# Cross attention of a perceiver block: text probabilities and weighted sums carried in the same turn and the same return transfer as the image probabilities, queries made per batch

## The chip, the cores and the metric

One Trainium2 chip, one of its cores. The metric is the device time of the whole program in microseconds (us); the kernel before has a median of 2453.11 us over 3 runs (2441.91 to 2453.33). The program computes a whole two-layer block; the change touches one stage of it, `cross_attention`, the image and text cross attention of the second layer.

## The reference, cut to what matters

```python
# x: 16 batches x 64 tokens x 256; context: 16 x 1601 x 256, the first 77 rows are text
def _attend(q, k, v):
    sim = jnp.einsum('bihd,bjhd->bhij', q, k) * SCALE        # 16 heads of 64, SCALE = 1/8
    attn = jax.nn.softmax(sim, axis=-1)
    out = jnp.einsum('bhij,bjhd->bihd', attn, v)
    return out.reshape(B, N, H * D)
q = (x @ Wq).reshape(B, N, HEADS, DIM_HEAD)
out = _attend(q, ctx_txt @ Wk, ctx_txt @ Wv)                  # 77 text keys
out = out + _attend(q, ctx_img @ Wk_ip, ctx_img @ Wv_ip)      # 1524 image keys
return out @ Wo + bo
```

Two softmaxes over two sets of keys, each normalised by itself, are added, and the sum goes through one output projection. All is fp32.

## The kernel before

The 1024 tokens are 8 tiles of 128, a tile is 2 batches of 64, and 16 heads are 8 pairs. The loop runs over 128 steps g; a step is one batch and one pair of heads (128 rows: 2 heads x 64 tokens), 16 steps to a tile. The image keys and values are never made: the query is taken through the key weights (`key_side`, result `a_hi` + `a_lo`), multiplied with the raw context (`ct`, split in two parts that one pass can hold exactly), and the probabilities are multiplied with the raw context rows (`cn`), after which the 256-wide sums go through the value weights (`value_side`).

Each engine has its own program, in order, and they meet in semaphores. In step g:

- PE (TensorE) computes the text scores and the image scores of g (L2237, L2248 to L2250: 18 matmuls of 508 columns), turns the normalised text probabilities of g-1 (`turn_text`, L2257) and the sums of g-3 (`turn_sums`, L2279), makes the key side of g+1 (L2228), then the sums of g-2 (L2271: 12 blocks, each three matmuls of 256 columns: `pt_hi` with both parts of `cn`, `pt_lo` with the first), and the value side of g-3 (L2293, L2295). The scores of g+1 wait until ScalarE has read the scores of g (`exp_done`).
- DVE (VectorE) takes the maxima (L2449, L2450), makes `a_lo` (L2437), turns the 128x1536 probabilities within 32x32 blocks in four instructions (L2466), normalises the text (L2470), splits the moved probabilities (`pt_lo`, L2478) and keeps the sums (L2482).
- ACT (ScalarE) computes the exponentials (L2402, L2405), copies `pt_hi` from `prob_moved` (L2414), and keeps what PE leaves in three PSUM banks that go round (`t_ps`).
- POOL (GpSimd) splits the context of the next batch as it is loaded.
- SP issues the transfers. A block turned within 32x32 is not yet turned as a whole; the rest of the turn is a trip through memory. Four stores (L2147) go out, one after each of the four DVE instructions, each from all 128 partitions in runs of 1536 bytes; then four returns (L2152), each into 32 partitions, again in runs of 1536 bytes. The landing place `prob_moved` has two buffers, so the returns of g wait for the splits of g-2. After them SP issues one load of context and, in some steps, weights and text keys and values.

Every 16 steps comes a boundary: the queries of the next tile (L2218: 16 fp32 products with 128 columns, 32 matmul records) are made between score steps, and key side and scores wait for them. Two steps later the finished tile goes through the output projection (`project`, L2307). `wq` and `wo` share one place in SBUF (`w_shared`) and are loaded in turn.

Of the kernel before, what the change touches and what calls it, by code (L numbers as in the profile page):

```python
# [22 lines left out]
P = 128  # L23
D = 256
# [2010 lines left out]
def cross_attention(nc, k, src, first):  # L2035
# [8 lines left out]
    RUN = IB * QR  # L2044
    with ExitStack() as ctx:
# [19 lines left out]
        prob = sb("prob1", [P, TXT + IB * P])  # L2065
        blocks = sb("prob_blocks", [P, Q, IB, QR])
# [3 lines left out]
        pt_txt = [sb(f"pt_txt{s}", [P, P]) for s in range(3)]  # L2070
        pairs = sb("pairs1", [P, 10, 2])
        top, bias, total, inv = ([pairs[:, at + s] for s in range(n)] for at, n in ((0, 2), (2, 2), (4, 3), (7, 3)))
        o = sb("o1", [P, D])
        ot = sb("ot1", [P, C, P])
# [5 lines left out]
        k_in, v_in, v_used = sem("k_txt_in"), [sem(f"v_txt_in{b}") for b in range(2)], sem("v_txt_used")  # L2080
# [4 lines left out]
        turned, moved_in, split_done = sem("prob_turned"), [sem(f"prob_moved_in{s}") for s in range(2)], sem("prob_split")  # L2085
        t_done = [sem(f"t1_done{j}") for j in range(RING)]
        t_kept = [sem(f"t1_kept{j}") for j in range(RING)]
        a_hi_kept, pt_hi_kept, txt_normed = sem("a_hi_kept"), sem("pt_hi_kept"), sem("txt_normed")
        summed, half_summed, inv_done, sums_kept = sem("summed1"), sem("half_summed1"), sem("inv1_done"), sem("sums1_kept")
        q_zeroed, pad_zeroed = sem("q_zeroed"), sem("prob_pad_zeroed")  # L2090
        stored = [sem(f"prob_stored{m}") for m in range(Q)]
# [7 lines left out]
        def boundary(g):  # L2099

            return g % STEPS == STEPS - 1 and g < N - 1

        def projects(g):

            return g // STEPS - 1 if g % STEPS == 2 and g >= STEPS else None
# [5 lines left out]
        def _(sp):  # L2111
# [29 lines left out]
            for g in range(N):  # L2141
# [12 lines left out]
                if g // PAIRS1 + 1 < NB:  # L2154
                    load(g // PAIRS1 + 1, g % PAIRS1)
                if n == 0 and i:
                    sp.wait_ge(scored, g)
                    load_keys(i, 1)
                    sp.wait_ge(queried, i + 1)
                    sp.dma_start(wo, src["wo1"]).then_inc(wo_in, 16)  # L2160
                if n == 4 and i:
                    sp.wait_ge(v_used, 2 * i)
                    load_values(i, 1)
                if n == 5 and 1 <= i < NT - 1:
                    sp.wait_ge(projected, i)
                    sp.dma_start(wq, src["wq1"]).then_inc(wq_in, 16)
                if n == 12 and i < NT - 1:
                    sp.wait_ge(scored, i * STEPS + 12)
                    load_keys(i + 1, 0)
                if n == 13 and i < NT - 1:  # L2170
                    sp.wait_ge(v_used, 2 * i + 1)
                    load_values(i + 1, 0)

        @block.gpsimd
        def _(pool):
# [14 lines left out]
            nc.gpsimd.memset(prob[:, TXT + IMG:], 0.0).then_inc(pad_zeroed, 1)  # L2190
# [8 lines left out]
        def _(pe):  # L2199
# [11 lines left out]
            def queries(t):  # L2211

                for side in range(2):
                    bank = use()
                    for j in range(4):
                        p = 4 * side + j
                        for c in range(C):
                            last = nc.tensor.matmul(t_ps[bank][:, j * P:(j + 1) * P], wq[:, c, p * P:(p + 1) * P],  # L2218
                                                    k.h_t[:, c, t * P:(t + 1) * P], start=c == 0, stop=c == C - 1)
                    last.then_inc(t_done[bank], 1)  # L2220
                return ring.place(2), ring.place(1)
# [31 lines left out]
            def turn_text(g):  # L2253

                bank = use()
                pe.wait_ge(txt_normed, g + 1)
                nc.tensor.transpose(t_ps[bank][0:TXT, 0:P], prob[:, 0:TXT], k.ident).then_inc(t_done[bank], 1)  # L2257

            def sums(g):
# [15 lines left out]
            def turn_sums(g):  # L2275
                bank = use()
                pe.wait_ge(sums_kept, g + 1)
                for c in range(C):
                    last = nc.tensor.transpose(t_ps[bank][:, c * P:(c + 1) * P], o[:, c * P:(c + 1) * P], k.ident)  # L2279
                last.then_inc(t_done[bank], 1)  # L2280
                return ring.place(1)

            def value_side(g):
# [3 lines left out]
                if p == 0:  # L2287
                    pe.wait_ge(v_in[b], 16 * i + 16)
                heads = [(t_ps[bank][r * S:(r + 1) * S, 0:S], slice((2 * p + r) * HD1, (2 * p + r + 1) * HD1),
                          slice(r * S, (r + 1) * S)) for r in range(2)]  # L2290
                for c in range(C):
                    for out, cols, rows in heads:
                        nc.tensor.matmul(out, wv[:, c, cols], ot[:, c, rows], start=c == 0, stop=False)  # L2293
                for out, cols, rows in heads:
                    last = nc.tensor.matmul(out, v_txt[0:TXT, b, cols], pt_txt[g % 3][0:TXT, rows],  # L2295
# [3 lines left out]
            def project(t):  # L2299
                kept(ring.place(1))  # L2300
                if t < NT - 1:
                    pe.wait_ge(wo_in, 16 * (t + 1))
# [9 lines left out]
            q_places = queries(0)  # L2312
            pe.wait_ge(wk_in, 16)
            for place in q_places:
                kept(place)
            a_place = key_side(0)
            for g in range(N + 3):
# [10 lines left out]
                if boundary(g):  # L2328
                    if g > STEPS:
                        pe.wait_ge(wq_in, 16 * (g // STEPS) + 16)  # L2330
                    q_places = queries(g // STEPS + 1)
                elif g < N - 1:
                    a_place = key_side(g + 1)
                if 2 <= g <= N + 1:
                    sums(g - 2)
                if boundary(g):
                    for place in q_places:
                        kept(place)
                    a_place = key_side(g + 1)
                if g >= 3:  # L2340
                    if g == 3:
                        pe.wait_ge(wv_in, 16)
                    kept(ot_place)
                    value_side(g - 3)
                if projects(g) is not None:
                    project(projects(g))
# [9 lines left out]

        def keep_queries(eng, copy, mine, ring):

            for side in range(2):
                bank, count = ring.next()  # L2360
                if side == mine:
                    eng.wait_ge(t_done[bank], count)
                    for r in range(2):
                        rows = slice(r * HD1, (r + 1) * HD1)
                        last = copy(q[rows, 4 * side:4 * side + 4, :, r, :],
                                    t_ps[bank][rows, :].rearrange("p (j b n) -> p j b n", j=4, b=2))
                    last.then_inc(t_kept[bank], 1)
# [9 lines left out]
        def _(act):  # L2377
# [9 lines left out]

            act.wait_ge(q_zeroed, 1)
            keep_queries(act, copy, 0, ring)
            keep_a(0)  # L2390
            for g in range(N + 3):
                if 1 <= g <= N:
                    keep(act, copy, ring, pt_txt[(g - 1) % 3][0:TXT, :], TXT, P)
                if g >= 3:
                    keep(act, copy, ring, flat(ot), P, D)
                if not boundary(g) and g < N - 1:
                    keep_a(g + 1)
                if g < N:
                    act.wait_ge(bias_done, g + 1)
                    if g:  # L2400
                        act.wait_ge(turned, Q * g)
                    nc.scalar.activation(prob[:, TXT:M].rearrange("p (j m) -> p j m", j=SB), s_ps[:, 1:4, 0:SBLK],  # L2402
# [625 lines left out]
```

## Time and profile before

| | |
|---|---|
| median of 3 runs | 2453.11 us (2441.91 to 2453.33) |
| profiled execution | 2435.73 us, of it the span 2433.6 us |
| first to last score step in the span | 624.1 to 2000.7 us |
| PE busy over the span | 2160.2 us (89%) |
| DVE, ACT, POOL busy | 65%, 38%, 36% |
| DMA engines, mean share | 48.1% for the queue that SP issues on |

PE's records overlap, so what a piece of its work takes is read from the start of one record to the start of the next. The cross attention takes 1.4 ms of the 2.4 ms. Outside it nothing is changed.

### The profile page before, as it was taken

How to read it: one execution, taken by the hardware profiler on the slowest of the kernel's cores; microseconds unless marked ns; L12 is line 12 of the kernel's file. 1: busy time of each engine (PE TensorE's matmuls, PEld its weight loads, DVE VectorE, ACT ScalarE, POOL GpSimd, SP SyncE). 2: the span in 40 equal slices, each digit the busy share in tenths (PEclk: the TensorE clock that was granted, in tenths of full speed). 3: DMA queues.
4: the chain of work that ended last, by engine and by line, in shares of the span. 5: the costliest groups of instructions: out<-in, count | busy, mean ns of one | idle time of the engine just before them, and what ended most of it. 6: DMA issues, size and time to landing. Idle time of an engine off the chain costs nothing. (4 is left out here: it accounts for less than half of the span.)

```text
span 2433.6 us, 37422 instructions
## 1 busy us (share of the span) xinstructions
PE 2160.2 (89%) x13637; PEld 1726.1 (71%) x13637; DVE 1570.4 (65%) x2756; ACT 925.0 (38%) x1869; POOL 877.5 (36%) x535
## 2 busy tenths in 40 slices
PE   5878877796699999999999999999999997787897
PEld 3445545464598889888898998998998994334684
DVE  4179934333577677677677677777776763795554
ACT  1166611210244344344344444444443443452331
POOL 1066412431343333243343333343333300362455
PEclk8989977798899999999999999999999998798898
DMA  5800002511476677677676777776776656001364
GB/s 159 169 16 14 8 1 88 230 50 57 145 200 184 185 218 205 185 217 206 185 217 180 226 202 208 198 207 199 202 211 186 194 156 248 4 0 44 98 148 114
DMA packets 229957, 362.99 MB, mean 149 GB/s; under 512 B 41920, under 2 KB 197824, under 8 KB 225168
## 3 DMA queue, kind: packets, MB, share of 16 engines
q1 hardware_dynamic: 223008, 342.08, 48.1%
q0 software_dynamic: 6768, 18.49, 3.2%
q8 instruction: 115, 1.88, 0.3%
q14 instruction: 66, 0.54, 0.1%
HBM read 234.97 MB, written 125.50 MB: 148 GB/s over the span
## 5 line engine op out<-in xcount | busy, mean ns | idle before, releaser
L2271 PE MATMUL img_ps<-cn,pt_hi 128*128 128x256 f32 (+1 forms) x3072 | 569.7, 287 | 3.0 <-DVE pt_lo L2478 3.0
L2271 PEld LDWEIGHTS img_ps<-cn,pt_hi 128*128 128x128 f32 (+1 forms) x3072 | 477.3, 191 | 3.2 <-issue 3.2
L2271 PE MATMUL img_ps<-cn,pt_lo 128*128 128x256 f32 (+1 forms) x1536 | 435.9, 284 | 0.0
L2466 DVE STREAM_TRANSPOSE prob_blocks<-prob 128x384 f32<-128x384 f32 x512 | 250.6, 547 | 183.8 <-ACT prob L2402 175.9
L2248 PE MATMUL s_ps<-ct,a_hi 128*128 128x508 f32 x768 | 315.7, 411 | 0.0
L2249 PE MATMUL s_ps<-ct,a_hi 128*128 128x508 f32 x768 | 304.2, 396 | 0.0
L2250 PE MATMUL s_ps<-ct,a_lo 128*128 128x508 f32 x768 | 304.0, 396 | 0.0
L2001 POOL TENSOR_SCALAR ct<-staged 128x762 fp32r<-128x762 f32 x64 | 136.8, 2138 | 439.6 <-DMA staged<-in_ctx_t 312.5
L2271 PEld LDWEIGHTS img_ps<-cn,pt_lo 128*128 128x128 f32 (+1 forms) x1536 | 292.6, 190 | 0.0
L2478 DVE TENSOR_TENSOR pt_lo<-prob_moved,pt_hi 128x768 fp32r<-128x768 f32 x256 | 277.9, 1124 | 9.4 <-ACT pt_hi L2414 9.2
L2001 POOL TENSOR_SCALAR cn<-staged 128x768 fp32r<-128x768 f32 x64 | 137.4, 2147 | 376.5 <-DMA staged<-in_ctx_n 293.4
L2379 ACT ACTIVATE pt_txt<-t_ps 77x128 f32<-77x128 f32 x128 | 34.9, 273 | 577.0 <-PE t_ps L2257 577.0
L2402 ACT ACTIVATE prob<-s_ps,pairs 128x1524 f32<-128x1524 f32 x128 | 196.5, 1535 | 136.7 <-DVE pairs L2453 136.7
L2414 ACT ACTIVATE pt_hi<-prob_moved 128x768 fp32r<-128x768 f32 x256 | 214.7, 842 | 62.7 <-PE img_ps L2271 46.7
L2450 DVE TENSOR_REDUCE pairs<-s_ps 128x1 f32<-128x1524 f32 x128 | 222.0, 1735 | 0.0
L2250 PEld LDWEIGHTS s_ps<-ct,a_lo 128*128 128x128 f32 x768 | 146.5, 191 | 32.6
L2249 PEld LDWEIGHTS s_ps<-ct,a_hi 128*128 128x128 f32 x768 | 147.6, 192 | 27.3
L2248 PEld LDWEIGHTS s_ps<-ct,a_hi 128*128 128x128 f32 x768 | 147.3, 192 | 27.5
L1736 PE MATMUL up_ps_b<-up_all_m,xt_b 128*128 x436 | 152.4, 481 | 1.3 <-issue 0.5
L2449 DVE TENSOR_REDUCE pairs<-s_ps 128x1 f32<-128x77 f32 x128 | 30.4, 238 | 182.9 <-PE s_ps L2250 182.9
L2003 POOL TENSOR_TENSOR cn<-staged,cn 128x768 fp32r<-128x768 f32 x64 | 125.6, 1963 | 5.3
L1684 POOL DMA_INDIRECT rows_b<-rows_m,token_m x86 | 84.7, 984 | 113.4 <-POOLq L1467 64.1
(370 smaller groups left out, 3712.9 us busy)
## 6 DMA issues: line engine op xcount, KB each, us to landing
prob_rows<-prob_blocks SPq DMA_DIRECT2D x512, 192.0 KB, 2.1
prob_moved<-prob_rows SPq DMA_DIRECT2D x512, 192.0 KB, 3.6
staged<-in_ctx_n SPq DMA_DIRECT2D x64, 384.0 KB, 4.7
staged<-in_ctx_t SPq DMA_DIRECT2D x64, 381.0 KB, 4.7
up_all_m<-in_up SPq DMA_DIRECT2D x8, 2048.0 KB, 12.8
down_all_m<-in_down SPq DMA_DIRECT2D x8, 1024.0 KB, 23.4
sums_m<-y_b SPq DMA_DIRECT2D x63, 128.0 KB, 2.2
w_shared<-in_wq SPq DMA_DIRECT2D x7, 1024.0 KB, 7.3
```

What stands on the lines that cost most here:

```text
L1736: last = nc.tensor.matmul(up_ps[j % 2][:, own], xt[j % 2][:, c, :], m.up[:, bass.ds(expert, 1), c, own].rearrange("p a h -> p (a h)"), sta ...
L2001: nc.gpsimd.tensor_scalar(hi, piece, 1.0, None, ALU.mult).then_inc(first.hi_done, 1)
L2003: nc.gpsimd.tensor_tensor(lo, piece, hi.bitcast(F32), ALU.subtract).then_inc(done, 1)
L2248: nc.tensor.matmul(out, a_hi[:, c, :], ct[b][:, 0, c, cols], start=c == 0, stop=False)
L2249: nc.tensor.matmul(out, a_hi[:, c, :], ct[b][:, 1, c, cols], start=False, stop=False)
L2250: last = nc.tensor.matmul(out, a_lo[:, c, :], ct[b][:, 0, c, cols], start=False, stop=c == C - 1)
L2271: last = nc.tensor.matmul(img_ps[:, 0:D], left[0:n, j, :], rows[0:n, right, j, :], start=j == 0 and at == 0, stop=j == IB - 1 and at == 2)
L2402: nc.scalar.activation(prob[:, TXT:M].rearrange("p (j m) -> p j m", j=SB), s_ps[:, 1:4, 0:SBLK], ACT.Exp, bias=bias[g % 2][:, 1:2], scale= ...
L2414: nc.scalar.activation(in_quarters(pt_hi, h), by_block(moved[(g - 1) % 2], h), ACT.Copy).then_inc(pt_hi_kept, 1)
L2450: nc.vector.tensor_reduce(top[g % 2][:, 1:2], s_ps[:, 1:4, 0:SBLK], mybir.AxisListType.XY, ALU.max).then_inc(topped, 1)
L2466: nc.vector.transpose(blocks[:, m], source[:, m]).then_inc(turned, 1)
L2478: nc.vector.tensor_tensor(in_quarters(pt_lo, h), by_block(moved[(g - 1) % 2], h), in_quarters(pt_hi, h).bitcast(F32), ALU.subtract).then_i ...
```

## The change

What it does:

- `prob` has 15 blocks of 128 columns in place of the 77 text columns and 12 image blocks: 12 of image probabilities, one of text probabilities (77 of its 128 columns), two of the 256-wide sums. Text and sums in it are those of two steps earlier.
- One DVE instruction turns all 1920 columns. The four stores now take a quarter of the partitions each (32 partitions, four runs of 1920 bytes from each), all after that instruction. One return brings everything to 128 partitions, 7680 bytes to each. `prob_moved` has one buffer in place of two; the return of g waits for the splits of g-1 and the value side of g-4.
- PE's `turn_text` and `turn_sums` go, with ACT's copies of their results. The value side reads text and sums from `prob_moved`, a step later than before, and waits for the return of the step before its own. 
- The sums take two matmuls to a block in place of three: `pt_hi` with both parts of `cn` (512 columns), `pt_lo` with the first. ACT scales the second half (`o_part`) and DVE adds. ACT, not DVE, normalises the text.
- Queries are made per batch (64 columns, 16 products) at the end of steps 6 and 13 of a tile, and ACT keeps them. `wq` and `wo` are loaded in halves, in steps 4 and 5 and in 14 and 15.

```diff
-    RUN = IB * QR
+    TXT_AT, O_AT = IB, IB + 1
+    BUNDLE = IB + 1 + C
+    RUN = BUNDLE * QR
+    LAG = 3
...
-        block_rows = nc.dram_tensor("prob_rows", (2, Q, P, RUN), F32).ap()
-        moved = [sb(f"prob_moved{s}", [P, Q, IB, QR]) for s in range(2)]
+        block_rows = nc.dram_tensor("prob_rows", (2, Q, QR, Q, RUN), F32).ap()
+        moved = sb("prob_moved", [P, Q, BUNDLE, QR])
...
+        def queries_of(g):
+
+            i, _, _, n = parts(g)
+            return {6: 2 * i + 1, 13: 2 * i + 2 if i < NT - 1 else None}.get(n) if g < N else None
...
         # sync
                 if g >= 2:
-                    sp.wait_ge(moved_in[s], 16 * Q * (g // 2))
-                for m in range(Q):
-                    sp.wait_ge(turned, Q * g + m + 1)
-                    sp.dma_start(block_rows[s, m], blocks[:, m].rearrange("p j r -> p (j r)")).then_inc(stored[m], 16)
-                if g >= 2:
-                    sp.wait_ge(split_done, 2 * (g - 1))
-                for m in range(Q):
-                    sp.wait_ge(stored[m], 16 * (g + 1))
-                    sp.dma_start(moved[s][m * QR:(m + 1) * QR].rearrange("c a j r -> c a (j r)"),
-                                 block_rows[s, m].rearrange("(a c) f -> c a f", a=Q)).then_inc(moved_in[s], 16)
+                    sp.wait_ge(moved_in, 16 * (g - 1))
+                sp.wait_ge(turned, g + 1)
+                for a in range(Q):
+                    sp.dma_start(block_rows[s, :, :, a].rearrange("m c f -> c m f"),
+                                 blocks[a * QR:(a + 1) * QR].rearrange("c m j r -> c m (j r)")).then_inc(stored[a], 16)
+                if g:
+                    sp.wait_ge(split_done, 2 * min(g, N))
+                if g > LAG:
+                    sp.wait_ge(valued, g - LAG)
+                for a in range(Q):
+                    sp.wait_ge(stored[a], 16 * (g + 1))
+                sp.dma_start(moved[:].rearrange("p a j r -> p (a j r)"),
+                             block_rows[s].rearrange("m c a f -> (m c) (a f)")).then_inc(moved_in, 16)
...
         # tensor
-                        for at, (left, right) in enumerate(((pt_hi, 0), (pt_hi, 1), (pt_lo, 0))):
-                            last = nc.tensor.matmul(img_ps[:, 0:D], left[0:n, j, :], rows[0:n, right, j, :],
-                                                    start=j == 0 and at == 0, stop=j == IB - 1 and at == 2)
+                        nc.tensor.matmul(img_ps[:], pt_hi[0:n, j, :], rows[0:n, :, j, :], start=j == 0, stop=False)
+                        last = nc.tensor.matmul(img_ps[:, D:2 * D], pt_lo[0:n, j, :], rows[0:n, 0, j, :],
+                                                start=False, stop=j == IB - 1)
...
             def value_side(g):
+                pe.wait_ge(moved_in, 16 * (g + LAG + 1))
...
-            for g in range(N + 3):
+            for g in range(N + LAG + 2):
...
-                if 1 <= g <= N:
-                    turn_text(g - 1)
-                if g >= 3:
-                    ot_place = turn_sums(g - 3)
...
+                if LAG + 1 <= g <= N + LAG:
+                    value_side(g - LAG - 1)
+                    head_place = ring.place(1)
+                if queries_of(g) is not None:
+                    if g >= STEPS:
+                        pe.wait_ge(wq_in, 32 * (g // STEPS) + 16)
+                    q_place = queries(queries_of(g))
...
         # vector
-                    for m in range(Q):
-                        if g:
-                            dve.wait_ge(stored[m], 16 * g)
-                        nc.vector.transpose(blocks[:, m], source[:, m]).then_inc(turned, 1)
+                    if g:
+                        for a in range(Q):
+                            dve.wait_ge(stored[a], 16 * g)
+                    nc.vector.transpose(blocks[:], prob[:].rearrange("p (j m c) -> p m j c", j=BUNDLE, m=Q)).then_inc(turned, 1)
```

## Rows read from the trace of the kernel before

**Rows 1.** The page, part 1: busy time (share of span) xinstructions.

```profile
PE 2160.2 (89%) x13637; PEld 1726.1 (71%) x13637; DVE 1570.4 (65%) x2756; ACT 925.0 (38%) x1869; POOL 877.5 (36%) x535
```

**Rows 2.** Windows (A:B length, busy by engine, PEclk, DMA share, GB/s), steps.

```profile
660.00:2000.00 1340.00, 1318.02 (x9770) 1191.89 (x9770) 976.63 (x1647) 582.20 (x1258) 489.95 (x241) 0.99 0.69 199
```

**Rows 3.** Waits of 660 to 2010: who waited for whom, total us, times, longest.

```profile
PE s_ps L2237 <- issue: 11.8, 7, 1.9
DVE prob_blocks L2466 <- ACT prob L2402: 172.8, 125, 1.7
```

**Rows 4.** Timeline of PE, one step: start, us, what, count.

```profile
1199.71 0.45 PE L2237 MATMUL s_ps<-k_txt,q 128*128 128x77 f32 x2
1199.95 0.47 PE L2248 MATMUL s_ps<-ct,a_hi 128*128 128x508 f32 x1
...
1204.16 0.27 PE L2257 MATMUL t_ps<-small,prob 128*77 128x128 f32 x1
...
1204.49 0.61 PE L2228 MATMUL t_ps<-q,wk 128*128 128x128 f32 x4
1204.85 0.49 PE L2271 MATMUL img_ps<-cn,pt_hi 128*128 128x256 f32 x2
...
1209.33 0.45 PE L2293 MATMUL t_ps<-ot,wv 128*64 128x64 f32 x8
...
1209.83 0.45 PE L2237 MATMUL s_ps<-k_txt,q 128*128 128x77 f32 x2
```

**Rows 5.** Timeline of PE around a boundary and around a projection.

```profile
1136.04 0.45 PE L2237 MATMUL s_ps<-k_txt,q 128*128 128x77 f32 x2
1140.86 3.74 PE L2218 MATMUL t_ps<-h_t,w_shared 128*128 128x128 f32 x32
1152.19 0.68 PE L2237 MATMUL s_ps<-k_txt,q 128*128 128x77 f32 x2 [1.53 <-issue]
...
1186.00 3.84 PE L2307 MATMUL t_ps<-w_shared,head_out 128*128 128x128 f32 x32 [0.55 <-ACT head_out L2379]
```

**Rows 6.** Timeline of VectorE in the same step as rows 4.

```profile
1200.24 1.82 DVE L2478 TENSOR_TENSOR pt_lo<-prob_moved,pt_hi 128x768 fp32r<-128x768 f32 x2
1204.52 1.74 DVE L2450 TENSOR_REDUCE pairs<-s_ps 128x1 f32<-128x1524 f32 x1
1208.14 1.96 DVE L2466 STREAM_TRANSPOSE prob_blocks<-prob 128x384 f32<-128x384 f32 x4 [1.36 <-ACT prob L2402]
```

**Rows 7.** Timeline of SP in the same step: stores, then returns.

```profile
1208.80 1.81 SPq L2147 DMA_DIRECT2D prob_rows<-prob_blocks  x4
1210.73 1.84 SPq L2152 DMA_DIRECT2D prob_moved<-prob_rows  x4
```

**Rows 8.** Tile view, single issues: store at 1208.80, returns at 1210.73 and 1212.27.

```profile
DMA to landing us min/median/max: 1.9/1.9/1.9
...
DMA to landing us min/median/max: 3.3/3.3/3.3
...
DMA to landing us min/median/max: 4.4/4.4/4.4
```

**Rows 9.** Windows: stores alone; returns alone; a context load and a weight load.

```profile
1209.75:1211.75 2.00, 2.00 (x15) 1.66 (x12) 1.96 (x5) 0.65 (x2) 1.92 (x2) 1.00 1.03 368
...
1213.25:1215.25 2.00, 2.00 (x15) 1.75 (x14) 1.44 (x4) 0.60 (x2) 0.00 (x0) 1.00 0.90 199
...
1226.75:1228.00 1.25, 1.25 (x13) 1.25 (x12) 0.27 (x1) 1.25 (x1) 0.00 (x0) 1.00 0.97 397
```

**Rows 10.** DMA issues: tensors, count, KB each, median us from issue to landing.

```profile
staged<-in_ctx_n SPq DMA_DIRECT2D x64, 384.0 KB, 4.7
...
w_shared<-in_wq SPq DMA_DIRECT2D x7, 1024.0 KB, 7.3
...
x_sb<-in_x SPq DMA_DIRECT2D x1, 1024.0 KB, 5.9
...
wv<-in_wv SPq DMA_DIRECT2D x1, 1024.0 KB, 4.7
```

**Rows 11.** Score steps by line (first and last start), and the last projection.

```profile
L2237 PE MATMUL s_ps<-k_txt,q x256: 232/275/497, 624.1 to 2000.9; 128*128 128x77 f32 x128
...
2029.48 3.84 PE L2307 MATMUL t_ps<-w_shared,head_out 128*128 128x128 f32 x32 [0.32 <-ACT head_out L2379]
```

More of the change, by code:

```diff
@@ L2097, in parts @@
             return i, n // PAIRS1, n % PAIRS1, n
[L2099 to L2101 removed]
+        def queries_of(g):
+            i, _, _, n = parts(g)
+            return {6: 2 * i + 1, 13: 2 * i + 2 if i < NT - 1 else None}.get(n) if g < N else None
         def projects(g):
[L2105 removed]
+            return g // STEPS - 1 if g % STEPS == LAG + 1 and g >= STEPS else None
         def half(h):
@@ L2209, in kept, with queries @@
                 pe.wait_ge(t_kept[place[0]], place[1])
[L2211 to L2221, printed above, removed]
+            def queries(b):
+                bank = use()
+                for p in range(PAIRS1):
+                    for c in range(C):
+                        last = nc.tensor.matmul(t_ps[bank][:, p * S:(p + 1) * S], wq[:, c, p * P:(p + 1) * P],
+                                                k.h_t[:, c, b * S:(b + 1) * S], start=c == 0, stop=c == C - 1)
+                last.then_inc(t_done[bank], 1)
+                return ring.place(1)
             def key_side(g):
@@ L2311, in _ @@
             pe.wait_ge(wq_in, 16)
-            q_places = queries(0)
+            q_place = queries(0)
             pe.wait_ge(wk_in, 16)
-            for place in q_places:
-                kept(place)
+            kept(q_place)
             a_place = key_side(0)
-            for g in range(N + 3):
+            for g in range(N + LAG + 2):
                 if g < N:
@@ L2355, in flat @@
             return a[:].rearrange("p c n -> p (c n)")
[L2357 to L2367, printed above, removed]
         def by_block(tile, h):
@@ L2386, in keep_a, with keep_queries @@
                 nc.scalar.activation(flat(a_hi), t_ps[bank][:, 0:D], ACT.Copy).then_inc(a_hi_kept, 1)
+            def keep_queries(b):
+                bank, count = ring.next()
+                act.wait_ge(t_done[bank], count)
+                act.sem_inc(queried, 1)
+                for r in range(2):
+                    rows = slice(r * HD1, (r + 1) * HD1)
+                    last = copy(q[rows, :, b % 2, r, :], t_ps[bank][rows, :].rearrange("p (j n) -> p j n", j=PAIRS1))
+                last.then_inc(t_kept[bank], 1)
             act.wait_ge(q_zeroed, 1)
-            keep_queries(act, copy, 0, ring)
+            keep_queries(0)
             keep_a(0)
[L2391 to L2396, printed above, removed]
+            for g in range(N + LAG + 2):
+                if g < N - 1:
                     keep_a(g + 1)
+                if projects(g) is not None:
+                    ring.next()
+                    ring.next()
                 if g < N:
@@ L2440, in _ @@
             nc.vector.memset(q[:], 0.0).then_inc(q_zeroed, 1)
-            dve.wait_ge(q_zeroed, 1)
-            keep_queries(dve, copy, 1, ring)
-            dve.sem_inc(queried, 1)
+            ring.next()
             keep_a_lo(0)
             dve.wait_ge(pad_zeroed, 1)
-            for g in range(N + 3):
+            for g in range(N + LAG + 2):
                 if g < N:
@@ L2484, in _ @@
-                if boundary(g):
-                    keep_a_lo(g + 1)
-                if g >= 3:
-                    ring.next()
                 if projects(g) is not None:
-                    if g == STEPS + 2:
+                    if g == STEPS + LAG + 1:
                         dve.wait_ge(bo_added, 1)
@@ L2496, in _ @@
                     dve.sem_inc(projected, 1)
+                if 1 <= g <= N:
+                    for h in range(2):
+                        dve.wait_ge(pt_hi_kept, 2 * (g - 1) + h + 1)
+                        nc.vector.tensor_tensor(in_quarters(pt_lo, h), by_block(moved, h),
+                                                in_quarters(pt_hi, h).bitcast(F32), ALU.subtract).then_inc(split_done, 1)
+                if 2 <= g <= N + 1:
+                    dve.wait_ge(part_kept, g - 1)
+                    dve.wait_ge(turned, g + 1)
+                    nc.vector.scalar_tensor_tensor(out=prob[:, O_AT * P:], in0=img_ps[:, 0:D],
+                                                   scalar=inv[(g - 2) % 3][:, 1:2], in1=o_part[:], op0=ALU.mult,
+                                                   op1=ALU.add).then_inc(sums_kept, 1)
+                if LAG + 1 <= g <= N + LAG:
+                    ring.next()
+                if queries_of(g) is not None:
+                    ring.next()
 class ScanWeights:
```

158 lines of the change are left out of this document (65 added, 93 removed).

## The prediction

> **What bounds the kernel now.** I read the page's busy shares first, then the windows, then the waits, then one step in the timeline of each engine. PE is busy 89% of the span [rows 1], and between 660 and 2000 us 1318.02 of 1340 us, at 0.99 of its clock [rows 2]. What it waits for there is small: 11.8 us in 7 places [rows 3], the tile boundaries. So the score loop is bound by PE's own stream of matmuls. An ordinary step lasts 1209.83 - 1199.71 = 10.12 us [rows 4]. A boundary step lasts 1152.19 - 1136.04 = 16.15 [rows 5], 6.03 more: 3.7 for the queries, the rest waiting. A projection adds 3.84 and a wait of 0.55, less 0.1 of overlap: 4.3 [rows 5]. A tile of 16 steps is 16 x 10.12 + 6.03 + 4.3 = 172.3 us. The 127 steps from 624.1 to 2000.7 us [rows 11] are 7.9 tiles.
>
> VectorE has slack: it waits 172.8 us in 125 steps before it turns the probabilities [rows 3]. The transfers of a step are done long before anybody needs them: the stores go out at 1208.80, the returns at 1210.73 [rows 7], and the last, issued at 1212.27, lands 4.4 later [rows 8], at 1216.67; ScalarE first wants them in the next step, after its exponentials, near 1218.4. That slack is what the change spends.
>
> **What PE saves.** The turns of text and sums take 1204.49 - 1204.16 = 0.33 us [rows 4]; they go. The 36 matmuls of the sums take 1209.33 - 1204.85 = 4.48, 0.124 each. The 508-column matmuls come at (1204.16 - 1199.95)/18 = 0.234 [rows 4], so a block of 512 and 256 columns costs 0.236 + 0.124 = 0.360 in place of 0.373: 0.16 over 12 blocks. PE's own work per step becomes 10.12 - 0.33 - 0.16 = 9.63. The queries leave the boundary and its 2.3 us of waiting; their work stays. With 64 columns a record costs between half of today's 3.74/32 = 0.117 [rows 5] and all of it, if the weight load sets the pace: 1.9 to 3.7 us for each batch. I take 2.4, since a projection record with its whole 128 columns is no quicker than 0.12.
>
> **What joins the path.** The value side of step k-4 stands at the end of PE's step k, and now waits for the return of k-1. PE is in order, so the scores of k+1 stand behind it. Nobody waited there before. I follow one bundle from the start S of its score step:
> - DVE starts to turn at S + 1208.14 - 1199.71 = S + 8.43 [rows 4, 6]. That is unchanged.
> - The turn: 1920 columns for 1536. Four pieces take 1.96 [rows 6], so 1.25 x 1.96 = 2.45; by the reduction's rate (1524 columns in 1.74, rows 6) 2.19. I take 2.3. Before, the first store left after one quarter, at 1208.80; now all four leave after the whole, 0.12 behind it: S + 10.85.
> - The stores, W. A store of 192 KB from 128 partitions lands 1.9 after issue [rows 8]; the window of stores alone moves 368 GB/s [rows 9], so 0.53 of that is data and 1.37 is latency. Each new store has 240 KB (245,760 bytes), but leaves only 32 partitions. No row shows such a store. Its two neighbours: stores from 128 partitions (0.67 us each at 368 GB/s, W = 1.37 + 4 x 0.67 = 4.05), and today's returns, which touch 32 partitions of SBUF: 199 GB/s in a window of their own [rows 9], and by their landings (1216.67 - 1214.03)/3 = 0.88 us for 192 KB [rows 7, 8]. Scaled to 240 KB that is 1.10 to 1.24; with 1.17, W = 1.37 + 4.68 = 6.05. I take 6.05: the 32 partitions are what the new stores share with that row, and HBM as such isn't what slows those returns, since context and weights come in at 397 GB/s [rows 9].
> - The return, L: 960 KB to all partitions. The nearest loads of 1024 KB land after 4.7 to 7.3 us [rows 10], the 7.3 with others queued ahead. The queue is empty when this one is issued, because SP has waited for the stores: 4.5, range 4.0 to 5.9.
> - From landing to the next scores: 0.1 and the value side, 1209.83 - 1209.33 = 0.50 [rows 4]. With 0.1 for SP's wait: 0.7 in all.
>
> So the scores of step g+2 can't start before S + 10.85 + W + L + 0.7, and two steps last 11.55 + W + L. With 6.05 and 4.5 that is 22.1: T = 11.05 us a step, against 9.63 of PE work and 10.12 today. The gain on PE becomes a wait of 1.4 us in front of every value side.
>
> A rule of the Trainium skill speaks against these stores. The page "SBUF — State Buffer", section "Door 1: The DMA port swizzle", says that a transfer's bandwidth depends on how many of SBUF's 16 ports its partitions reach, that 32 neighbouring partitions reach 8, and gives 189 GB/s at 1 MiB for them. By its figure (an estimate from that page) a store would have 1.30 us of data, W would be 6.6 and T 11.3. The trace agrees for transfers into 32 partitions, with its 199 GB/s [rows 9]; no run here shows it for transfers out of them.
>
> **Per tile, the extras.** Queries come right behind the value side and so on the path of one of the two alternating chains, twice a tile: 2.4 in all. Those of step 6 also wait for the second half of `wq`, which SP issues in step 5 behind return and context load: about 2 on one chain, so 1.0. A projection of 3.84 eats the slack of 1.4 and costs 2.4 on one chain and 1.0 on the other: 1.7. The halves of `wq` and `wo` (1.4 us of data at 368 GB/s, four times) and text keys and values are queued behind a context load, and the next stores behind them, by about 1.0 and 0.6: half of the sum, 3.2. Together 8. A tile is 16 x 11.05 + 8 = 184.8, 12.5 more than 172.3; over 7.9 tiles +99 us.
>
> **The end.** From the last scores (2000.7, rows 11) to the last projection's end it is 33 us. Now four bundles must still go round: the first lands at 10.85 + 6.05 + 0.1 + 4.5 = 21.5, and each further one 8.45 later (turn and stores, because one `prob_blocks` holds the next turn until the stores have landed): 46.9, plus value side and projection 5: 52. That is +19.
>
> DVE loses the text scaling and gets 0.3 more of turn and a little more for the sums: nothing, since it waits anyway. ACT gets two small operations and loses two: nothing; but what it does after its wait for the return (splits, sums, values) comes 1.7 to 3 us after the landing, and the next sums are wanted 5.5 after it, so this stays hidden, with POOL's collisions too. The single buffer costs nothing by itself, since the splits are done about 3 us after a landing and the stores of the next bundle land 5.5 after it.
>
> **Sum.** The profiled execution has 2435.7 us (span 2433.6). 2435.7 + 99 + 19 = 2554. The median of the runs is 17 above that execution, the fastest run 6. I predict 2560.
>
> **Rivals.**
> - The stores run at the full rate: W = 4.05, L = 4.5, T = 10.05. A tile is 160.8 + 10 (less slack, so queries and projection show more) = 170.8; -1.5 x 7.9 = -12; the end +13. With L at 4.0 T is 9.8 and the whole -30. Time 2410 to 2455, say 2425. For it: no row shows a slow store. Against: the returns' 199 GB/s. From W + L = 8.7 (T = 10.12) down it decides. Chance 0.17.
> - The change does what its instruction counts say: PE stays the bound, T = 9.65, a tile 154.4 + 8.7 = 163, -9.2 x 7.9 = -73, the end +8: 2375. It needs W + L under 7.8, less than 4.05 + 4.0. Against it is the sum of its two fastest rows. Chance 0.07.
> - The added wait is larger than my sum: PE's pauses let the clock go down, or the loads of context (4.7 alone, rows 10) and weights meet the stores in each step and W + L reaches 12.5: T = 12, a tile 202, +235: 2690. Half of that, 2620, is nearer. For it: 7.3 where a load had company. Against: the clock stayed at 0.99 over boundaries with 2 us of waiting [rows 2, 5]. Chance 0.12.
> - The forecast: 0.64, by itself 2500 to 2600.
>
> About 0.5% (12 us) is what a measurement of this kernel tells from no change. Faster: 0.22 (second rival, most of the first); same: 0.05; slower: 0.73. The range is 2415 to 2630.
>
> **What would show it.** Right: PE waits about 1.4 us in nearly every step before L2293's successor, released by the DMA of `prob_moved`; steps near 11 us; in the stores' window about 210 GB/s with the last landing 6 us after the first issue; the return landing in 4.5; no wait at the boundary; PE's busy share down, not the number of GB/s. Wrong: stores of 240 KB that land 0.7 us apart, or a value side that never waits and steps of 9.7; or a PE that waits elsewhere, at the scores for the exponentials or at the sums for the splits, which would mean that ACT or DVE, behind the return, sets the step.

## The result, and the profile after

The changed kernel takes 2693.12 us (median of 4 runs, 2687.21 to 2701.5), the kernel before 2452.89 (4 runs). The ratio is 1.0994, 95% interval 1.0948 to 1.104: 9.9% slower. The forecast was 2560 us, 4.4% slower, with a range that ended at 2630. The sign, the wait that joins the path and the length of the round trip at the full clock came out as forecast; the size did not.

The waits of PE in the score loop. Each row: who waited for whom, total us, times, longest. It answers to [rows 3].

```profile
PE t_ps L2288 <- DMA prob_moved<-prob_rows: 154.0, 62, 5.0
PE t_ps L2226 <- DMA w_shared<-in_wq: 14.0, 7, 2.2
PE img_ps L2272 <- DVE prob L2471: 6.2, 4, 2.5
```

L2288 is the value side. Where PE waited 11.8 us before, at boundaries, it now waits 154 us for the return. Two steps of PE's timeline, against [rows 4]:

```profile
1215.34 0.45 PE L2288 MATMUL t_ps<-prob_moved,wv 128*64 128x64 f32 x8
...
1215.84 0.45 PE L2245 MATMUL s_ps<-k_txt,q 128*128 128x77 f32 x2
...
1227.80 0.45 PE L2288 MATMUL t_ps<-prob_moved,wv 128*64 128x64 f32 x8 [2.65 <-DMA prob_moved<-prob_rows]
...
1228.30 0.45 PE L2245 MATMUL s_ps<-k_txt,q 128*128 128x77 f32 x2
```

This step lasts 12.46 us in place of 10.12, and 2.65 of it is one pause ahead of the value side. VectorE's turn and SP's timeline in the same step, against [rows 6, 7]:

```profile
1214.55 2.18 DVE L2448 STREAM_TRANSPOSE prob_blocks<-prob 128x1920 f32<-128x1920 f32 x1 [1.36 <-ACT prob L2385]
```

```profile
1216.80 2.71 SPq L2150 DMA_DIRECT2D prob_rows<-prob_blocks  x4
1222.91 0.34 SPq L2158 DMA_DIRECT2D prob_moved<-prob_rows  x1
```

The turn takes 2.18 us. From the first store's issue to the return's, which waits for the last store, it is 6.11 us in this step; over the steps of the loop the median is 5.98, with the last store landing 5.90 after the first issue. The page's rows of the transfers (count, KB each, median us to landing):

```profile
prob_rows<-prob_blocks SPq DMA_DIRECT2D x524, 240.0 KB, 4.1
prob_moved<-prob_rows SPq DMA_DIRECT2D x131, 960.0 KB, 4.8
```

And the window of the loop (length, busy by engine, PEclk, DMA share, GB/s), against [rows 2]:

```profile
660.00:2220.00 1560.00, 1393.41 (x8121) 1178.34 (x8120) 908.27 (x1128) 590.48 (x1268) 514.87 (x240) 0.92 0.66 203
```

PEclk is the line that the forecast got wrong. 0.92 over 1560 us means, with two levels of 1.2 and 2.4 GHz, 0.08 x 1560 / 0.5 = 250 us at half clock, where the kernel before had some 27 by the same sum (0.01 x 1340 / 0.5), and 17 by the single stretches of its trace. It comes in two ways. In the ordinary steps the wait mostly falls into every second step only, and the scores of the step after it often start at half clock. The step that begins at 1239.82 has 1.72 us of waiting just ahead of it. PE, the clock over its first scores, and VectorE's turn:

```profile
1239.33 0.45 PE L2288 MATMUL t_ps<-prob_moved,wv 128*64 128x64 f32 x8 [1.72 <-DMA prob_moved<-prob_rows]
...
1239.82 0.45 PE L2245 MATMUL s_ps<-k_txt,q 128*128 128x77 f32 x2
```

```profile
1240.30:1243.60 3.30, 3.30 (x9) 2.57 (x9) 2.64 (x3) 1.21 (x4) 3.18 (x2) 0.50 0.94 275
```

```profile
1249.83 2.18 DVE L2448 STREAM_TRANSPOSE prob_blocks<-prob 128x1920 f32<-128x1920 f32 x1 [1.36 <-ACT prob L2385]
```

The turn starts 10.01 us after the scores, where it starts 8.42 after them in a step at the full clock (1214.55, with scores from 1206.13). The round trip starts later by that much, and PE itself does not wait in this step, because its slow scores have used up the time. Where it hurts most is step 6 of a tile, the one with queries and their weights just reloaded:

```profile
1297.54 0.45 PE L2245 MATMUL s_ps<-k_txt,q 128*128 128x77 f32 x2
...
1309.32 0.45 PE L2288 MATMUL t_ps<-prob_moved,wv 128*64 128x64 f32 x8 [2.46 <-DMA prob_moved<-prob_rows]
...
1311.92 7.09 PE L2226 MATMUL t_ps<-h_t,w_shared 128*128 128x64 f32 x32 [2.02 <-DMA w_shared<-in_wq]
1318.80 0.65 PE L2245 MATMUL s_ps<-k_txt,q 128*128 128x77 f32 x2
```

```profile
1311.90:1318.80 6.90, 6.88 (x33) 6.89 (x33) 1.03 (x2) 0.00 (x0) 2.95 (x2) 0.50 0.73 238
1318.80:1324.70 5.90, 5.90 (x21) 4.89 (x22) 0.00 (x0) 1.19 (x2) 2.95 (x2) 0.72 0.29 102
```

Two pauses, 2.46 and 2.02 us, with half a microsecond of work between; then the granted clock is 0.50 for all 32 query records (7.09 us), and 0.72 over the next scores. The step lasts 21.26 us. Summed over the places of a tile (medians over the 8 tiles, from the starts of L2245), a tile takes 199.6 us: 11.5 for each of 13 ordinary steps, 21.3 and 14.9 for the steps with queries, 13.4 for the one with the projection. Before it was 172.3, the forecast 184.8.

Where the 253 us of the profiled spans (2686.7 against 2433.6) are: the loop from the first scores (621.6) to the last (2223.4) has 225 more; from there to the last projection's end 53.7 us in place of 32.6, which is 21; the other stages 7.

### The profile page after: what moved, and what is told of

Read it like the earlier page. It is cut to its first block and busy times, and to the rows that moved or that the text cites. A ratio compares the mean times of both kernels' runs of the same rounds, so it can differ in the third digit from the quotient of the medians.

```text
span 2686.7 us, 34018 instructions
## 1 busy us (share of the span) xinstructions
PE 2243.5 (84%) x11973; PEld 1720.1 (64%) x11973; DVE 1507.7 (56%) x2231; ACT 937.2 (35%) x1885; POOL 905.4 (34%) x535
## 5 line engine op out<-in xcount | busy, mean ns | idle before, releaser
L2272 PE MATMUL img_ps<-cn,pt_hi 128*128 128x512 f32 (+1 forms) x1536 | 560.4, 406 | 13.7 <-DVE pt_lo L2466 7.4
L2448 DVE STREAM_TRANSPOSE prob_blocks<-prob 128x1920 f32<-128x1920 f32 x131 | 285.3, 2178 | 189.7 <-ACT prob L2385 170.9
L2466 DVE TENSOR_TENSOR pt_lo<-prob_moved,pt_hi 128x768 fp32r<-128x768 f32 x256 | 296.5, 1197 | 136.2 <-ACT pt_hi L2397 136.1
L2256 PE MATMUL s_ps<-ct,a_hi 128*128 128x508 f32 x768 | 343.8, 448 | 0.0
L2272 PEld LDWEIGHTS img_ps<-cn,pt_hi 128*128 128x128 f32 (+1 forms) x1536 | 290.9, 189 | 79.3 <-issue 7.6
L2257 PE MATMUL s_ps<-ct,a_hi 128*128 128x508 f32 x768 | 330.0, 430 | 0.0
L2258 PE MATMUL s_ps<-ct,a_lo 128*128 128x508 f32 x768 | 326.9, 426 | 0.0
L2361 ACT ACTIVATE a_hi<-t_ps 128x256 fp32r<-128x256 f32 x128 | 49.3, 385 | 526.6 <-PE t_ps L2236 526.6
L2288 PE MATMUL t_ps<-prob_moved,wv 128*64 128x64 f32 x1024 | 60.7, 240 | 170.6 <-DMA prob_moved<-prob_rows 170.5
L2256 PEld LDWEIGHTS s_ps<-ct,a_hi 128*128 128x128 f32 x768 | 164.4, 214 | 33.1
L2257 PEld LDWEIGHTS s_ps<-ct,a_hi 128*128 128x128 f32 x768 | 163.6, 213 | 32.2
L2288 PEld LDWEIGHTS t_ps<-prob_moved,wv 128*64 128x64 f32 x1024 | 44.4, 143 | 204.9 <-issue 204.9
```

The lines of the kernel that those rows point to most:

```text
L2256: nc.tensor.matmul(out, a_hi[:, c, :], ct[b][:, 0, c, cols], start=c == 0, stop=False)
L2257: nc.tensor.matmul(out, a_hi[:, c, :], ct[b][:, 1, c, cols], start=False, stop=False)
L2258: last = nc.tensor.matmul(out, a_lo[:, c, :], ct[b][:, 0, c, cols], start=False, stop=c == C - 1)
L2272: nc.tensor.matmul(img_ps[:], pt_hi[0:n, j, :], rows[0:n, :, j, :], start=j == 0, stop=False)
L2448: nc.vector.transpose(blocks[:], prob[:].rearrange("p (j m c) -> p m j c", j=BUNDLE, m=Q)).then_inc(turned, 1)
L2466: nc.vector.tensor_tensor(in_quarters(pt_lo, h), by_block(moved, h), in_quarters(pt_hi, h).bitcast(F32), ALU.subtract).then_inc(split_done, 1)
```

## The experiments

All ratios are to the kernel before, run on the same chip.

**e1_all_partitions.** Is it the 32 partitions?

```diff
-                    sp.dma_start(block_rows[s, :, :, a].rearrange("m c f -> c m f"),
-                                 blocks[a * QR:(a + 1) * QR].rearrange("c m j r -> c m (j r)")).then_inc(stored[a], 16)
+                    sp.dma_start(block_rows[s, a].rearrange("c a f -> (c a) f"),
+                                 blocks[:, a].rearrange("p j r -> p (j r)")).then_inc(stored[a], 16)
```

> The changed kernel with its four stores made as before the change from all 128 partitions (one quarter of the columns each, 1920 bytes from each partition) in place of 32 partitions with four runs each. Same bytes, same number of transfers; the bytes land in other rows of the DRAM buffer, so the probabilities are permuted and the output is not the reference's. Port theory (stores from 32 partitions run at about half rate and the bundle's round trip sets the step): from the first store's issue to the last landing 4.1 us in place of 5.9; two steps last 11.55 + 4.1 + 4.8 = 20.4, so ordinary steps near 10.2 in place of 11.7, the granted clock in the loop up from 0.92 to 0.97 or more, total 2450 to 2530. Rival (the stores are slow because all four leave at once, or because of the DRAM side): 5.9 us stay, total within 1% of 2693.

Measured 2528.16 us, ratio 1.0354 (1.032 to 1.0388). SP's timeline, then the transfers, then the window of the loop:

```profile
1209.35 1.79 SPq L2150 DMA_DIRECT2D prob_rows<-prob_blocks  x4
1213.33 0.32 SPq L2158 DMA_DIRECT2D prob_moved<-prob_rows  x1
```

```profile
prob_rows<-prob_blocks SPq DMA_DIRECT2D x524, 240.0 KB, 2.5
prob_moved<-prob_rows SPq DMA_DIRECT2D x131, 960.0 KB, 4.8
```

```profile
660.00:2070.00 1410.00, 1334.11 (x8130) 1130.26 (x8131) 916.51 (x1135) 591.15 (x1270) 515.74 (x241) 0.97 0.63 224
```

3.98 us in place of 6.11, with the same bytes in runs of the same length; ordinary steps near 10.5 and less time at half clock. One half of the rival is out: it isn't that all four leave at once. The other half, the DRAM side, is not settled by this run alone, because the edit changes that side too: a store now writes one contiguous stretch, where the change's writes rows that lie 7680 bytes apart. e6 below leaves each store as it is and still gains, which speaks for the partitions. The two ends of the forecast's bound for W, 4.05 and 6.05, are close to the two kernels' values, 3.93 and 5.90 from the first issue to the last landing (medians).

**e2_filled_pause.** Is it the clock?

```diff
+                for _ in range(FILL if g + LAG + 1 < N else 0):      # FILL = 3
+                    nc.tensor.matmul(t_ps[bank][:, 0:2 * P], k.ident, wv[:, 0, 0:2 * P], start=True, stop=True)
                 pe.wait_ge(moved_in, 16 * (g + LAG + 1))
```

> The changed kernel with three fp32 matmuls of 256 columns (about 1.3 us at the full clock, results overwritten) put on PE just before the wait of the value side for the return. Clock theory (the pauses let the granted clock fall to half in one stretch after another, 253 us of the loop at half clock, and the slow stretches cost more than the pauses themselves): clock in the loop 0.97 or more, ordinary steps fall from 11.7 towards the 11.15 that the round trip of the bundle allows, the step with the queries from 21 to 16 or less, total 2590 to 2640. Rival (the clock is a by-product, the round trip alone sets the steps): within 0.7% of 2693, or slower where the extra matmuls come late.

Measured 2636.75 us, ratio 1.0799 (1.0764 to 1.0833). Two rows of PE's timeline (L2285 is the filler) and the window:

```profile
1206.98 1.46 PE L2285 MATMUL t_ps<-wv,small 128*128 128x256 f32 x6
1208.37 0.45 PE L2291 MATMUL t_ps<-prob_moved,wv 128*64 128x64 f32 x8
...
1218.03 1.46 PE L2285 MATMUL t_ps<-wv,small 128*128 128x256 f32 x6
```

```profile
660.00:2180.00 1520.00, 1482.08 (x8872) 1251.15 (x8873) 927.21 (x1136) 596.76 (x1274) 521.57 (x241) 0.98 0.70 209
```

PE has 1.39 us more to do in each step, and the kernel is some 50 us faster. The steps are 11.05 us long. That PE now just fills them is the choice of the filler's size, so the equality with the forecast's 11.05 is no proof of it by itself; but the wait at the value side has shrunk to 19 us over the loop, so the round trip needs no more than 11.05 either. The clock went from 0.92 to 0.98. This supports the theory; the rival, no gain, is out. One part was missed: the step with the queries still takes 17.7 us, not 16 or less, because the pause for `wq` is not filled and half clock follows it there.

**e3_value_after_keys.** Is it the place of the wait? On PE:

```diff
                     a_place = key_side(g + 1)
+                if LAG + 2 <= g <= N + LAG + 1:
+                    value_side(g - LAG - 2)
+                    head_place = ring.place(1)
...
-                if LAG + 1 <= g <= N + LAG:
-                    value_side(g - LAG - 1)
-                    head_place = ring.place(1)
```

> The changed kernel with the value side moved on PE from the end of step k to just behind the key side of step k+1 (and ScalarE's copy of its result and the ring places with it); nothing else. The return then has 5 us more before PE waits for it. Theory (the place of this one wait made the round trip the bound): PE never waits at the value side, ordinary steps 9.7, only the query steps (3.6 us of PE work each, plus the wait for the query weights of about 2) and projections longer: a tile 16 x 9.7 + 7.2 + 3.9 + 2.5 = 169 against 172 before, total 2420 to 2460. Rival (the single landing buffer and ScalarE and VectorE behind the return are the next bound): PE waits for the splits at the sums, steps 10.3 to 11, total 2500 to 2600.

Measured 2547.15 us, ratio 1.0432 (1.0328 to 1.0535): outside the theory's 2420 to 2460 and inside the rival's 2500 to 2600. PE's waits from 660 to 2000 us:

```profile
PE img_ps L2272 <- DVE prob L2473: 32.3, 36, 2.5
PE t_ps L2226 <- DMA w_shared<-in_wq: 30.6, 6, 7.4
PE img_ps L2272 <- DVE pt_lo L2468: 8.1, 1, 8.1
```

The waits at the value side (151 of the 154 us lie in the loop) are gone, so the place of the wait was the cause of those pauses, as the theory says. But the stall did not vanish: PE waits for the sums that VectorE keeps behind its splits, which is the rival's mechanism, and longer for `wq`.

**e4_two_matmuls_only.** The part that should be good by itself, put into the kernel before: the `sums` loop of the change, with `o_part` in the place of `o`, on ScalarE and VectorE as the change has it.

> The kernel before with one part of the change: the sums in two matmuls a block (512 and 256 columns) in place of three of 256, ScalarE scaling the second half and VectorE adding. Theory (PE bound, 0.16 us a step saved): steps 9.96 in place of 10.12, total 18 to 22 us less than before, 2431 to 2436. Rival (the extra ScalarE operation comes between the splits and the sums kept, and VectorE's late finish in the steps with GpSimd contention makes PE wait): no change or up to 1% slower.

Measured ratio 0.9976 (0.996 to 0.9992); steps 10.04 us in place of 10.12. Run again, 12 times in place of 8:

> The kernel of e4_two_matmuls_only again, in more rounds: the kernel before with the sums in two matmuls a block. The first look gave a ratio of 0.998 to the kernel before. Theory (PE bound, 0.08 us a step saved): 0.995 to 0.998 of the kernel before, the interval below 1. Rival (the first look was noise): an interval that holds 1.

0.9985 (0.9964 to 1.0006): the interval just holds 1, so the rival isn't excluded by that run. In both profiles an ordinary step is 10.04 us. The gain, if it is one, is 0.15 to 0.24%, 4 to 6 us where 18 to 22 were expected first; in the length of a step it is 0.08 us in place of 0.16.

**e5_queries_early.** Is it the reload of `wq` ahead of step 6?

```diff
-            return {6: 2 * i + 1, 13: 2 * i + 2 if i < NT - 1 else None}.get(n) if g < N else None
+            return {13: 2 * i + 2, 15: 2 * i + 3}.get(n) if g < N and i < NT - 1 else None
```

with the loads of `wo` in steps 0 and 1 and of `wq` in steps 7 and 8.

> The changed kernel with the queries of both batches of a tile made at the end of steps 13 and 15 of the tile before, wo loaded in steps 0 and 1 and wq in 7 and 8, so that wq lies in SBUF long before it is wanted; nothing else. PE has the same matmuls. Theory (step 6 with its 21.3 us is a chain: pause for the return, pause of 2 us for wq, then 32 query records of 64 columns at half the clock, 7.1 us where the full clock takes 3.6, and the scores after them slow too): no PE wait for wq, the two query steps 14 to 16 us each in place of 21.3 and 14.9, total 50 to 60 us less than the changed kernel: 2635 to 2645. Rival (it is the query work itself, not the pause ahead of it): the slow step moves to another place, total within 0.7% of 2693.

Measured 2681.13 us, ratio 1.094 (1.0887 to 1.0992), some 12 us less and not told from no change. No wait for `wq` is left, but PE still waits 164.8 us in 72 places for the return, and the step of 21 us is now one of 18 at place 15. The expected 50 to 60 us did not come; the slow step moved to another place, as the rival has it. But the query work by itself is not what is slow: the queries of place 13 run at the full clock here in four of six tiles, and with the pauses filled (e9) those of both places do in all tiles but one. What fits both runs is that the pause ahead of the value side is enough to bring the clock down; the reload was a small part.

**e6_stores_two_queues.** Ports again, with the result unchanged. SP issues the stores of a = 0 and 1, and ScalarE, behind its exponentials:

```diff
+                    act.wait_ge(turned, g + 1)
+                    for a in range(Q // 2, Q):
+                        act.dma_start(block_rows[g % 2, :, :, a].rearrange("m c f -> c m f"),
+                                      blocks[a * QR:(a + 1) * QR].rearrange("c m j r -> c m (j r)")).then_inc(stored[a], 16)
```

> The changed kernel with the stores of partitions 64 to 127 issued from ScalarE's queue and those of 0 to 63 from SP's, so that both pairs are under way together; shapes, bytes and result as in the changed kernel. Port theory (a store from 32 partitions reaches half of the ports; partitions 0 to 63 one half, 64 to 127 the other): the two queues' stores use different ports, so from first issue to last landing 4.0 to 4.8 us in place of 5.9, steps 10.3 to 10.8, total 2530 to 2600. Rival (the 32 partitions limit a transfer in another way, or what is slow is the DRAM side): 5.5 or more, and ScalarE's time for the issues (0.9 us) comes on top: total 2680 to 2730.

Measured 2607.75 us, ratio 1.064 (1.0597 to 1.0684); 2530 to 2600 was expected, and steps of 10.3 to 10.8, where the median is 11.4. ScalarE's issues, then the page's rows:

```profile
1214.90 0.84 ACTq L2397 DMA_DIRECT2D prob_rows<-prob_blocks  x2
```

```profile
prob_rows<-prob_blocks ACTq DMA_DIRECT2D x262, 240.0 KB, 4.0
prob_rows<-prob_blocks SPq DMA_DIRECT2D x262, 240.0 KB, 3.8
```

The second store of a queue is issued 0.4 us after the first and lands 4.1 to 4.3 later, so the last of the four lands 4.7 us after the first issue (median), not 5.9, and the return goes out after 5.1, not 6.0. The rival's 5.5 or more is out, and since shapes and DRAM rows are those of the changed kernel, so is a limit that lies on the DRAM side alone. The first two land after 2.8 and 3.0 us, where the changed kernel's second lands after 4.0: one store from partitions 0 to 63 and one from 64 to 127 overlap. It is not all of e1's gain (3.9). Part of the gain went to a new wait, 82.6 us of PE for the sums, because ScalarE's copies come later.

**e7_late_value_order** and **e8_late_value_two_queues.** Can the change be mended? e7 has the value side of e3, the queries of e5, and `o_part`, text and sums kept ahead of the splits on ScalarE and VectorE. e8 adds e6. Both leave the fillers of e2 out.

> The changed kernel with three moves: the value side behind the key side of the next step, the queries of both batches at steps 13 and 15 with wq there early, and the sums and text kept (ScalarE, then VectorE) ahead of the splits, not behind them. All three theories together (place of the wait, the query chain, VectorE's late sums): PE bound again, steps 9.75, queries 3.6 twice, projection 4: a tile 16 x 9.75 + 11.5 = 167.5 against 172.3 before, minus 4.8 x 8 = 38, the end 10 more: 2415 to 2430, faster than before. Rival (the round trip bounds in another place, splits late for the sums): PE waits at the sums, steps 10.1 to 10.6, 2470 to 2540.

> The kernel of e7_late_value_order with the stores on two queues as in e6_stores_two_queues. If the stores take 4.5 us in place of 5.9, the return lands 1.4 us earlier and the splits end well before the sums: the same as e7_late_value_order or up to 1% faster, if that one still waits for splits. Rival: ScalarE waits for the turn before it can issue, its copies come later, and it is 0.5 to 2% slower than e7_late_value_order.

Measured 2484.13 us, ratio 1.0133 (1.0099 to 1.0166), and 2484.38, 1.0125 (1.0082 to 1.0168). e8 tells nothing from e7: with the wait out of the way the stores' speed no longer counts, and its own expectation of a loss did not come either. The loop of e7, and PE's waits:

```profile
660.00:2010.00 1350.00, 1300.43 (x8088) 1100.21 (x8086) 946.76 (x1134) 617.10 (x1267) 521.77 (x241) 1.00 0.74 234
```

```profile
PE s_ps L2245 <- ACT txt_prob L2397: 38.1, 36, 3.8
PE t_ps L2288 <- DMA prob_moved<-prob_rows: 21.6, 5, 7.7
PE img_ps L2272 <- DVE pt_lo L2478: 11.3, 14, 1.6
```

The clock is back at 1.00 without any fillers, and half of the places of a tile have steps of 9.75 to 9.9 us. Still it does not beat the kernel before: a tile comes to 172.8 us against 172.3. The 0.37 saved in each step (5.9 a tile) pays for the per-batch queries (2 x 3.6 against 3.7) and for scores that now wait for the exponentials, and the end is 23 us longer.

**e9_filled_and_early.** e2 and e5 together: what is left when the clock is held and `wq` is early?

> The changed kernel with both the filled pause (three fp32 matmuls ahead of the wait for the return) and the early queries (steps 13 and 15, wq loaded long before). Theory: what the forecast missed is the clock and the size of a query batch, nothing else. With the clock held, ordinary steps are 11.05, the length that the forecast's round trip gives, the query steps 3.6 longer and the projection step 3.5 longer: a tile 16 x 11.05 + 7.2 + 3.5 = 187.5 against 172.3 before, loop +121, end +21: total 2575 to 2600. Rival (another wait was missed): ordinary steps at 11.05, but over 195 us a tile, total 2630 or more.

Measured 2613.83 us, ratio 1.0657 (1.0623 to 1.069), between theory and rival: a tile of 188.3 us where 187.5 was expected, but some unsteady steps beside it. Two rows of a step with queries:

```profile
1175.03 3.79 PE L2227 MATMUL t_ps<-h_t,w_shared 128*128 128x64 f32 x32
1178.65 0.40 PE L2246 MATMUL s_ps<-k_txt,q 128*128 128x77 f32 x2
```

```profile
660.00:2140.00 1480.00, 1451.46 (x8823) 1223.23 (x8824) 933.40 (x1134) 594.23 (x1269) 524.09 (x241) 0.99 0.71 213
```

At the full clock a batch of queries takes 3.6 us to the start of the next scores. Its 32 records of 64 columns take 3.79 us, and the 32 of 128 columns in the kernel before took 3.74 [rows 5]: from start to start 0.113 and 0.112 us. Half the columns save nothing.

## Why the prediction was right or wrong

- **What PE saves.** Nearly right: 9.63 was forecast, 9.75 is the length of steps in which nobody waits (several places of the tile, in the changed kernel and in e7). The sums saved 0.08 in place of 0.16 (e4, e10).
- **The wait that joins the path.** Right, and it is where the forecast put it: the value side, for the return of the step before. e3 moves it and the 154 us are gone.
- **The stores.** W was forecast at 6.05, with the row of the 32-partition returns preferred to the row of the 128-partition stores; 5.90 was measured from the first issue to the last landing, and 3.93 with 128 partitions (e1). The rule quoted from the Trainium skill, "SBUF — State Buffer", section "Door 1: The DMA port swizzle", held for transfers out of 32 partitions as well; its own figure gave 6.6.
- **The return.** L: 4.5 forecast, 4.8 measured. The turn: 2.3 forecast, 2.18 measured.
- **The round trip.** Right at the full clock. With the measured terms, 10.7 to the first store (1216.80 is 2.25 after the turn's start, which is 8.42 after the scores), 6.1, 4.8 and 0.7 make 22.3 for two steps. Where no stretch at half clock lies in them, two ordinary steps of the changed kernel take 22.4 us (median of 14 pairs), and 22.3 with the pauses filled (e2, 60 pairs); 22.1 was forecast.
- **The step that failed: "DVE starts to turn at S + 8.43. That is unchanged", and with it the cost of the clock, put at nothing.** It was unchanged only while the clock was. From the fifth step of the loop on, 41 steps have more than 1 us at half clock in their first 4 us, and each of the 41 comes right behind a pause at the value side; of the pauses, two in three are followed so. In such ordinary steps the turn starts 10.0 us after the scores in place of 8.45, and two ordinary steps with a stretch at half clock last 23.6 us (46 pairs). That, more than the stores or the return, is why ordinary steps are 11.5 and not 11.05 on average. It also corrects one sign: the forecast had a wait of 1.4 us in nearly every step; there is one of some 2.5 in every second, because the slow scores use up the other. The steps at place 6 pay most, with queries of 7.1 us. Filling the pause (e2) is worth 1.0994 - 1.0799 = 0.0195, 48 us; with the wait for `wq` out too (e9) 0.034, 83 us, of which some is that wait itself and not the clock. The sum had no term for it. The forecast's excess was 0.044, the measured one 0.099.
- **The argument against it.** The third rival had it, "PE's pauses let the clock go down", and I gave that 0.12 because the clock had stayed at 0.99 over boundaries with 2 us of waiting. That 0.99 is an average over 1340 us with only 7 such pauses, and it hides what the clock did just behind them. After three of the seven the scores ran at half clock, after four they did not, and the boundary of [rows 5] is one of the three: its text scores take 0.68 us where those at the full clock take 0.45. The windows of the kernel before behind that boundary and behind another:

```profile
1151.70:1158.30 6.60, 6.11 (x16) 4.96 (x17) 0.39 (x2) 0.00 (x0) 3.04 (x2) 0.50 0.37 93
...
1498.50:1505.00 6.50, 6.50 (x39) 5.72 (x40) 1.89 (x2) 0.99 (x3) 3.97 (x2) 1.00 0.11 34
```

- **A figure that came true by luck.** That rival's time was 2690, and 2693 was measured. But 2690 was worked out from W + L = 12.5, which did not happen (5.9 + 4.8); it had no price for the clock either.
- **The queries.** Mis-sized: bounded between 1.9 and 3.7 us a batch, taken at 2.4, measured 3.6 at the full clock (e9), and at half clock 7.1. The upper bound, all of the 128-column record, was the right one. The projection step was 3.5 longer in e9, 1.7 was forecast; the loads behind each other cost less than the 3.2 forecast. Together 188.3 a tile in e9 in place of 184.8.
- **The end.** 52 us forecast, 53.7 measured.
- **What stays open.** e9 is at +161 us, the forecast's sum at +107 on the same measure. 39 of these 54 are in the loop (1514.5 us between first and last scores against 1376.6, so 138, where 99 were forecast), 28 of them the tile's 3.5 us; the rest is in single long steps and in the other stages, and no run separates them. Why a pause of 1.5 to 2 us is followed by half clock in one place and not in another stays open too.

## What to carry to other kernels

Follow one buffer through its whole round trip, and look where in its own program the engine that sets the pace will wait for it: two steps here had to hold 22 us of turn, stores and return, and 0.5 us less work per step bought nothing against that. When a tuned, TensorE-bound loop gets a pause in each step, price the pause and then the clock, and look at the clock just behind each pause and not at its mean over the loop: here it was worth a further 2% (e2). And when transfers are regrouped, count partitions on both sides; the change made the returns wide and the stores narrow, and the slow part only moved.

## What the runs showed of the hardware that was not expected

- Two stores from 32 partitions each, one in the lower and one in the upper half of the partitions, overlap when issued from two queues: four of them have landed 4.7 us after the first issue in place of 5.9 (e6). The Trainium skill's page "DMA: Bandwidth & Descriptors", section "Rules for kernel authors", says of transfers to disjoint partition halves that they serialize, from two queues too; here, for stores, they did not, though all from 128 partitions was faster still (3.9, e1).
- fp32 matmul records with a 128x128 weight tile follow each other after 0.113 us with 64 moving columns (e9) and after 0.112 with 128 (the queries of the kernel before): the number of columns makes no difference between those two.
- A pause of 2.46 us, half a microsecond of work and another pause of 2.02 us were followed by 7 us at a granted clock of 0.50; of the seven pauses of 1.5 to 1.9 us at the boundaries of the kernel before, three were followed by a granted clock of 0.50 and four by 1.00.
